# One more wait on GpSimd: rows of two choices landed ahead of a unit's fifth gather

## The reference, cut to what matters

```python
x = L0_attn_x                                   # (2, 2048, 256)
xn = _layernorm(x)
s = attn(xn)                                    # recurrence, gate, residual
_, idx = lax.top_k(biased, TOPK)                # TOPK = 4 of 16 experts
y = sum_over_experts(c_e * (silu_and_mul(xt @ w13_e.T) @ w2_e.T))
y = y + silu_and_mul(xt @ w13_s.T) @ w2_s.T     # shared expert
x = x + s * silu(y)
```

## Time and profile before

| | us |
|---|---|
| median of 3 runs | 537.93 |
| the three runs | 531.52, 537.93, 540.01 |
| the profiled execution, its own time | 532.27 |
| its span, first to last instruction | 530.2 |
| mean granted TensorE clock, share of full speed | 0.88 |

### The profile page before, as it was taken

How to read it: one execution, slowest core, us unless ns; L and a number is a source line. 1 busy time by engine, 2 the same in 40 slices (tenths; PEclk the granted TensorE clock), 3 DMA queues, 4 the chain that set the end, 5 groups by cost and what they waited for, 6 DMA issues and landing times.

```text
span 530.2 us, 11561 instructions
## 1 busy us (share of the span) xinstructions
PE 373.0 (70%) x3647; PEld 297.8 (56%) x3647; DVE 309.4 (58%) x923; ACT 283.6 (53%) x532; POOL 268.3 (51%) x280
## 2 busy tenths in 40 slices
PE   0467167779169999988989997988897786784210
PEld 0354144446048889877777786767775565563100
DVE  4889457448417535663556554877567464454744
ACT  1951346666227566656777875767565564443000
POOL 2004736667730055545566366665565664550774
PEclk9999667779659999999999998999899897887555
DMA  7997838886264679869988988989797887654554
GB/s 247 386 382 237 301 130 277 279 278 199 100 218 142 211 257 294 263 184 296 304 276 280 304 246 262 288 280 274 232 293 237 244 260 221 179 152 137 155 153 128
DMA packets 106586, 127.08 MB, mean 240 GB/s; under 512 B 10273, under 2 KB 95906, under 8 KB 106530
## 3 DMA queue, kind: packets, MB, share of 16 engines
q1 hardware_dynamic: 92560, 92.17, 54.1%
q0 software_dynamic: 12288, 33.57, 20.1%
q10 hardware_dynamic: 1682, 0.59, 0.4%
HBM read 59.71 MB, written 66.58 MB: 238 GB/s over the span
## 4 chain that ended last, share of the span: by engine, by line
PE 45%; DVE 19%; issue 13%; POOL 8%; another core or an unknown queue 6%; ACT 5%; DMA 3%; POOLq 0%; SPq 0%; DVEq 0%; ACTq 0%
PE bank L748 16%; PE bank L771 9%; PE bank L569 7%; POOL x_slots L529 4%; POOL xn_parts L550 4%; PE bank L676 3%; PE bank L761 3%; ACT xn_f L1489 2%; PE bank L662 1%; DVE xn_parts L1334 1%; DVE xn_f L1283 1%; DVE xn_parts L953 1%; DMA x_ring<-in_x 1%; PE bank L795 1%
## 5 line engine op out<-in xcount | busy, mean ns | idle before, releaser
L529 POOL DMA_INDIRECT x_slots<-xn_parts,slot_u x128 | 132.4, 1034 | 158.2 <-PE bank L569 72.8
L550 POOL DMA_INDIRECT xn_parts<-y_slots,slot_u x128 | 128.9, 1007 | 96.8 <-PE bank L569 33.3
L748 PE MATMUL bank<-w_all,xn_f 128*128 x1038 | 135.0, 280 | 9.8 <-issue 8.8
L748 PEld LDWEIGHTS bank<-w_all,xn_f 128*128 128x128 f16 x1038 | 100.0, 101 | 30.4 <-issue 17.3
L1283 DVE SCALAR_TENSOR_TENSOR xn_f<-bank,xn_f 128x256 f32<-128x256 f32 x88 | 36.9, 420 | 133.1 <-issue 68.1
L1603 ACT ACTIVATE xn_f<-bank 128x1024 f16<-128x1024 f16 x88 | 88.4, 1006 | 32.3 <-PE bank L569 23.2
L771 PE MATMUL bank<-w_all,sh_silu 128*128 x519 | 75.9, 284 | 13.7 <-issue 11.2
L1627 ACT ACTIVATE y_ring<-bank 128x512 f32<-128x512 f32 x88 | 52.0, 591 | 61.6 <-PE bank L771 30.3
L569 PE MATMUL bank<-ident_h,w_stage 128*128 128x128 f16 x692 | 55.7, 225 | 18.4 <-DMA w_stage<-x_slots 16.6
L771 PEld LDWEIGHTS bank<-w_all,sh_silu 128*128 128x128 f16 x519 | 47.7, 102 | 23.3 <-issue 16.2
L569 PEld LDWEIGHTS bank<-ident_h,w_stage 128*128 128x128 f16 x692 | 48.0, 101 | 20.8 <-DMA w_stage<-x_slots 16.8
(11 more groups left out here) (173 smaller groups left out, 468.3 us busy)
## 6 DMA issues: line engine op xcount, KB each, us to landing
w_stage<-x_slots SPq DMA_DIRECT2D x85, 256.0 KB
y_slots<-y_ring SPq DMA_DIRECT2D x85, 256.0 KB
x_ring<-in_x SPq DMA_DIRECT2D x32, 256.0 KB
x_slots<-zero_h SPq DMA_DIRECT2D x7, 896.0 KB
x_slots<-zero_h SPq DMA_DIRECT2D x1, 5120.0 KB, 21.7
x_slots<-zero_h SPq DMA_DIRECT2D x1, 4992.0 KB, 23.0
x_slots<-zero_h SPq DMA_DIRECT2D x7, 640.0 KB
w_stage<-in_w13t SPq DMA_DIRECT2D x17, 256.0 KB
```

The source lines that it names most:

```text
L529: eng.indirect_dma_start(out=x_slots[s], out_offset=bass.IndirectOffsetOnAxis(ap=slot_u[:, n * TOPK + k:n * TOPK + k + 1], axis=0), in_=xn ...
L550: eng.indirect_dma_start(out=fin_y[:, r, j, k, :], out_offset=None, in_=y_slots[s], in_offset=bass.IndirectOffsetOnAxis(ap=slot_u[:, n * T ...
L748: mm = eng.matmul(gu[:, j * 2 * F:(j + 1) * 2 * F], xg_T[:, n % 2, ((j * 2 + px) * KD + k) * P:((j * 2 + px) * KD + k + 1) * P], w_all[:, ...
```

## The change

Two lines are added in `gather_y`. In units 0 to 12, ahead of the gather of the third choice of the first tile (k = 2, j = 0, the fifth of eight), GpSimd waits until `y_in[r][1]` has the count of this unit: the two gathers of the second choice have then landed. The first choice's two gathers were issued ahead of them and have a semaphore of their own, for which it doesn't wait. Nothing is removed and nothing else moves.

```diff
@@ -547,6 +547,8 @@
                     if c < len(GATHER_PAIR):
                         i = k * FT + j
                         eng.wait_ge(pair_t, GATHER_PAIR[c] + i * GATHER_PAIRS[s] // (TOPK * FT))
+                    if c < len(GATHER_PAIR) and k == 2 and j == 0:
+                        eng.wait_ge(y_in[r][1], 16 * FT * (c // FIN_RING + 1))
                     eng.indirect_dma_start(
                         out=fin_y[:, r, j, k, :], out_offset=None, in_=y_slots[s],
                         in_offset=bass.IndirectOffsetOnAxis(ap=slot_u[:, n * TOPK + k:n * TOPK + k + 1], axis=0))\
```

## The result

The changed kernel takes 551.92 us (median of 4 runs, 550.72 to 552.71), the kernel before beside it 535.12 us: a ratio of 1.0335, 95% interval 1.0248 to 1.0422. Ratios count only the runs in the faster of the two states that a kernel's executions show, so they are not always the quotient of the medians. It is slower by 3.3%, just outside the range given, and on the side of the fourth rival. The profiled execution took 552.71 us, with a span of 550.4.

A forecast was written before the change was run, and what follows sets the result against it. The pair loop, held up beside unbroken runs of gathers, was taken as the bound. 13 us lost in units 0 to 7 less 10 gained in 8 to 12 gave +3 on 532.27, 540 on the median; range 528 to 550.

The forecast's parts named there:

- the fourth rival: Joined: at eight boundaries of units 0 to 8 runs grow to six and eight, 21 us against 10 gained; 549 us, chance 0.18.
- the wait binds in every unit: Ahead of each fifth gather the wait adds 1.4 to 2.5 us, about 26 us of GpSimd's time over 13 units, covered.
- nobody waits for the later rows: VectorE's combines use gathered rows much later (29 us in unit 10), so 2.5 us of delay are nothing there.
- So I take 2.7 each, 11 us, between 0 and 17.: Units 0 to 7: loss at four boundaries with a step of three pairs, each gaining two gathers in a run.
- I took 2.8 us from the tail: Landing time behind the fourth gather's end, read from unit 13 in the tail; ends 1.9 and 4 us.
- My own threshold for the fourth rival, 2.5 us: Rows landing later than this behind the fourth gather leave nothing separating fifth from seventh: unit 2's two idles, 1.45 + 1.02.
- Gain of this part: about 10 us, 5 to 14.: Units 8 to 12: the wait cuts runs into four and four with a pause of 2.8 us.
- my 2.0 us: Units 8, 10 and 11: price of two runs of four, against 4.7 us on average for a run of six.
- Hidden: Rival: the pair loop's loss has another reason, full DMA engines; cover absorbs the wait, both sums vanish; 538 us, chance 0.22.
- Broken everywhere: Rival: joined runs in units 0 to 7 start from empty queues, cost no more; only 10 us gain left; 528, chance 0.15.
- Its companion, fewer gathers in flight: Beside the third rival: fewer gathers in flight leave SP's loads and stores more DMA turns; same outcome, 528 us.

The follow-up runs named there:

- e9_join: Kernel before, no landing wait; in units 0 to 7 the third choice's gathers wait for the fourth's pair: 549.27 against 531.33 us, ratio 1.0345.
- e10_pause: Kernel before plus GpSimd memsets of about 0.9 us ahead of third, fifth and seventh gather of units 8 to 12: 519.32 against 531.33 us, ratio 0.9800.
- e14_four: Kernel before plus one 1.8 us memset ahead of the fifth gather of units 8 to 12: 527.58 against 530.87 us, ratio 0.9946.
- e1_late: Kernel before plus the landing wait only in units 10 to 12: 525.93 against 530.02 us, ratio 0.9931.
- e3_lag: Kernel before plus, ahead of each choice of units 0 to 12, a wait for landing of the choice before the last: 534.28 against 530.02 us, ratio 1.0037.
- e8_two: Kernel before plus the landing wait only in units 11 and 12: 477.66 against 477.5 us, ratio 0.9999.
- e11_busy: Kernel before plus eight GpSimd memsets in a row, 7 to 8 us, ahead of unit 11: 538.39 us in one run, against 531.33.

## Why the prediction was wrong

**Right.** What bounds the kernel: the pair loop, held up beside runs of gathers, and nothing in the tail. That the wait binds in every unit, that nobody waits for the later rows (no combine waited for rows ahead of the tail), and that it spends GpSimd's waits for pairs. That its effect goes by the runs and not by the wait: e9_join shows it without the wait, e10_pause with the opposite sign. The fourth rival named the outcome and the reason of the loss; its 10 us of gain in the late units were not there either.

**The step that failed, first: "So I take 2.7 each, 11 us, between 0 and 17."** The first gather of unit 8 starts at 430.66 us where it started at 410.41: units 0 to 7 cost 20 us, not 13, near the upper end of 21. Two things in it were mis-sized. I held that a stalled pair loop ends a run early; in unit 2 it didn't, and the run grew to eight, not six, at 7.8 us, where I had 1.0 + 2.7. And the landing was too short: I took 2.8 us from the tail, and GpSimd stood idle ahead of the fifth gather for 3.5 us on average and up to 5.43 (4.78 in unit 10, 3.50 in unit 8, 2.54 in unit 12), beyond my upper end of 4. The fixed 2.0 us plus bytes over 436e3 of the Trainium skill ("DMA: Bandwidth & Descriptors", "Anatomy of one DMA"), 2.3 us, is shorter than all of these. My own threshold for the fourth rival, 2.5 us, lay under my own value of 2.8; I should have given it the larger chance by that alone.

**Second: "Gain of this part: about 10 us, 5 to 14."** From the first gather of unit 8 to that of the tail are 80.4 us after and 80.9 before: the gain was 0.5 us. I had the runs end at the units' boundaries, as four and four. But unit 8's last gathers joined unit 9's, and unit 10's joined unit 11's. For this the delay within the unit is enough, without lateness from earlier ones: e14_four, with nothing changed before unit 8, has the same run of seven there, and e1_late, with nothing changed before unit 10, has the run of eight and a gain of 4.1 us. Nor were two runs of four as cheap as my 2.0 us: the one that I priced lost 1.0, but in the same trace the run of four from unit 4 into unit 5 has a pair gap of 5.60 us, 2.3 lost.

**Rivals.** *Hidden* fell with e9_join and e10_pause: the sends move the time both ways. *Broken everywhere* held that a pause with everything landed starts the next run afresh; the run of eight in unit 2 follows such a pause and costs 7.8 us. Its companion, fewer gathers in flight, got nothing from e3_lag's cap of four; whether fewer still would help, as the pauses of e10_pause make it, stays open.

**Left open.** Why TensorE's matmuls drip while GpSimd sends, in every session but one. The runs show that the sending brings it on there, and that it isn't the gathers' bytes or a GpSimd busy with memsets. What the sending acts through they don't show, nor whether pace or gathers in flight counts. Nor is it known what the session of 477.5 us had otherwise: the chip number is that of the next session. The changed kernel wasn't run in it. There the waits would find 3.3 us of cover at the end in place of 12.6, and the cost may be another; e8_two, with two of the thirteen waits, shows none (0.9999).

## What to carry to other kernels

A wait added to an engine with idle time isn't free because the idle time covers it: ask first what that idle time did. Here it parted the gathers, and a wait of 2.5 to 5.4 us ahead of the fifth took it from those behind. If a stall goes with bursts, pace the sends where they already burst (memsets of 0.9 us between twos in units 8 to 12: 2.0% faster than before here, 1.5% slower in the session without the stalls), and leave alone where they don't. Measure the price of a mechanism in more than one session, and on more than one chip, before building on it.

## What the runs showed of the hardware

- In every session but one TensorE's matmuls come in drips of one to four each 1.4 us beside an unbroken stream of indirect gathers from GpSimd, 1.25 us from one to the next. It lasts to about the end of the stream: 4.3 to 7.8 us lost with six to eight gathers in the changed kernel. The kernel before takes 530 us there. In that one session 68 gathers in a row cost nothing, and it takes 477.5 us: one kernel, 10% apart, and the same chip number in the record for that session and one of the others.
- Halving the bytes of the gathers changed nothing (ratio 1.0011), and 8 us of memsets on GpSimd did not disturb TensorE in the one trace that has them beside the stalls (e11_busy).
- Beside the pairs' transfers a fifth gather waited up to 5.4 us for the fourth to land, twice what the same wait shows in the tail (2.8).
